# One block for three stages: feed-forward's first weights loaded and split inside the last state-space step, and the softplus at other units

## The reference

```python
x = x + cross_attention(layernorm(x), ctx, wq, bq, wk, bk, wv, bv, wo, bo)   # 16 heads, 2048 keys
x = x + attn(layernorm(x), ...)        # state space, then an MLP
x = x + ffn(layernorm(x), ...)         # shared matrix + two weighted experts that share one matrix

def attn(Z):
    xs, z = split(Z @ in_proj_w.T)                         # 1024 channels each
    u = silu(causal_conv4(xs) + conv_b)
    dt_low, Bm, Cm = split(u @ x_proj_w.T)                 # 32 + 16 + 16
    dt = softplus(dt_low @ dt_proj_w.T + dt_proj_b)
    h[t] = exp(dt[t] * A) * h[t-1] + dt[t] * Bm[t] * u[t]  # 16 states per channel
    y = sum_n h[t, n] * Cm[t, n] + u * D
    Zm = rmsnorm((y * silu(z)) @ out_proj_w.T + Z, norm1_w)
    h1 = gelu(Zm @ mlp_w1.T + mlp_b1)                      # 2048 wide
    return rmsnorm(h1 @ mlp_w2.T + mlp_b2 + Zm, norm1_w)
```

## Time and profile before

| | |
|---|---|
| median of 3 runs | 4025.98 us (4024.71 to 4027.25) |
| profiled execution | 4028.83 us |
| its span, first to last instruction | 4027.1 us |
| granted TensorE clock, mean | 0.986 of full |
| PE busy | 3844.0 us, 95% |
| DVE busy | 2824.2 us, 70% |
| ACT busy | 1744.4 us, 43% |
| POOL busy | 1273.4 us, 32% |

### The profile page before, as it was taken

How to read it: one execution, slowest core, us unless ns; L and a number is a source line. 1 busy time by engine, 2 the same in 40 slices (tenths; PEclk the granted TensorE clock), 3 DMA queues, 4 the chain that set the end, 5 groups by cost and what they waited for, 6 DMA issues and landing times. The chain is left out here.

```text
span 4027.1 us, 83594 instructions
## 1 busy us (share of the span) xinstructions
PE 3844.0 (95%) x34880; PEld 2814.3 (70%) x34880; DVE 2824.2 (70%) x2977; ACT 1744.4 (43%) x3482; POOL 1273.4 (32%) x599
## 2 busy tenths in 40 slices
PE   8999999999999999999999998999999997699998
PEld 6777777877777777777777775555545553388886
DVE  5667667657667766766766766999999999654443
ACT  2324324414423433432442445776777767222221
POOL 1111111011011111111111103888888889521011
PEclk9999999999999999999999998999999999799999
DMA  4110110110010011111011022111211111220000
GB/s 154 38 43 29 38 43 28 38 53 31 28 50 31 29 51 37 35 38 43 28 38 43 28 83 89 53 30 45 63 58 58 32 42 48 76 74 22 32 23 20
DMA packets 96917, 183.73 MB, mean 46 GB/s; under 512 B 8465, under 2 KB 12945, under 8 KB 96562
## 3 DMA queue, kind: packets, MB, share of 16 engines
q1 hardware_dynamic: 96562, 178.27, 13.6%
HBM read 152.82 MB, written 25.43 MB: 44 GB/s over the span
## 5 line engine op out<-in xcount | busy, mean ns | idle before, releaser
L244 POOL TENSOR_TENSOR c_lo<-c_raw,c_hi 128x2048 fp32r<-128x2048 f32 x64 | 294.6, 4604 | 1973.8 <-DVE c_hi L346 1973.8
L434 DVE TENSOR_TENSOR prob_sums<-prob_sums,probs 128x1024 f32<-128x1024 f32 x480 | 566.6, 1222 | 116.4 <-ACT probs L319 116.4
L996 POOL TENSOR_TENSOR b_drive<-b_dt_u,b_bc 128x1024 f32<-128x1024 f32 x256 | 600.6, 2361 | 117.4 <-PE b_y L1433 83.6
L407 DVE TENSOR_REDUCE max_parts<-scores 128x2 f32<-128x1024 f32 x512 | 601.5, 1217 | 40.2 <-PE scores L571 40.2
L319 ACT ACTIVATE probs<-scores 128x512 f32<-128x512 f32 x1024 | 529.0, 603 | 216.3 <-PE scores L602 214.8
L399 DVE SCALAR_TENSOR_TENSOR k_lo<-scores,bk_sb,k_hi 128x512 fp32r<-128x512 f32 x256 | 192.2, 751 | 565.5 <-ACT k_hi L304 565.5
L1433 PE MATMUL b_y<-b_drive,b_ident 128*128 128x512 f32 x1024 | 501.9, 621 | 68.8 <-DVE b_drive L1296 40.1
L1285 DVE TENSOR_TENSOR_SCAN b_decay<-b_decay,b_drive 128x1024 f32<-128x1024 f32 x214 | 489.9, 2289 | 20.5 <-ACT b_decay L1151 18.9
L304 ACT ACTIVATE k_hi<-scores,bk_sb 128x512 fp32r<-128x512 f32 x256 | 176.4, 689 | 604.5 <-PE scores L523 604.5
L312 ACT COPY v_sb<-scores 128x512 f32<-128x512 f32 x240 | 141.2, 588 | 667.7 <-PE scores L523 667.7
L1151 ACT ACTIVATE b_decay<-b_dt,b_a 128x254 f32<-128x254 f32 x1024 | 425.3, 462 | 0.4
(11 more groups left out here) (232 smaller groups left out, 6518.5 us busy)
## 6 DMA issues: line engine op xcount, KB each, us to landing
c_raw<-in_ctx SPq DMA_DIRECT2D x64, 1024.0 KB, 5.1
b_bc<-bc_scratch SPq DMA_DIRECT2D x128, 256.0 KB, 4.4
q_scratch<-v_sb SPq DMA_DIRECT2D x4, 1024.0 KB, 4.3
q_raw<-q_scratch SPq DMA_DIRECT2D x16, 256.0 KB, 5.1
q_raw<-in_x SPq DMA_DIRECT2D x16, 256.0 KB, 2.8
x_scratch<-q_raw SPq DMA_DIRECT2D x16, 256.0 KB, 5.7
attn_scratch<-attn_out_sb SPq DMA_DIRECT2D x16, 256.0 KB, 2.0
b_attn<-attn_scratch SPq DMA_DIRECT2D x8, 512.0 KB, 5.5
```

Of the source, the lines that this page charges most:

```text
L244: pool.tensor_tensor(c_lo[:, slot], c_raw[:], c_hi[:, slot].bitcast(F32), ALU.subtract).then_inc(c_lo_ready, 1)
L407: dve.tensor_reduce(max_parts[:, g, 2 * pair:2 * pair + 2, s], max_banks[:, 2 * pair:2 * pair + 2, :], AX.X, ALU.max).then_inc(max_taken, 1)
L434: dve.tensor_tensor(part, part, probs[:, u % 4], ALU.add).then_inc(summed, 1)
L996: pool.tensor_tensor(drive[:, m % 4], dt_u[:, 2 * p:2 * p + 2, :].unsqueeze(1).to_broadcast([P, SG, 2, T]), bc[:, g, 0].unsqueeze(2).to_br ...
```

## The change

- The three stages are in one block. `feed_forward` returns its functions like the others. The last output projection, the last `add_input`, the squares, the weighing and the scaling of the last state-space step are handed to feed-forward's engine programs and are issued between its first instructions.
- In the last state-space step SP loads the eight pieces of `w1` (`load_first`, from unit 1 on), ACT makes the high parts (units 8 to 15, `high_w1`), POOL four low parts (units 14, 17, 20, 23) and the other four behind the loop. `b1` and the first two `zm` tiles are loaded after unit 25. The store of the `zm` of the step before the last (`zm_v[i - 1]`) stands behind all of these on SP.
- `w1`, `w2` and `w_shared` are split in place: the raw data lie where the low part goes. `w2` is loaded once the last unit is added, two pieces at a time, as before.
- To make room on POOL, the last step gives it four C products in place of seven (`POOL_C_LAST`).
- In every step `PE_DT`'s second half goes from unit 20 to 21, `take_t` from 21 and 24 to 22 and 25, the exponentials from 22 and 25 to 23 and 28, the rounding from 23 and 29 to 24 and 30, and POOL's first rounding error from 25 to 26.
- In attention the semaphore of the `bo` load is the one of the three other biases, so that ACT also waits for it before its first `take_queries`.

```diff
-            sp.dma_start(bo_rows[:], bo.partition_broadcast(P)).then_inc(bo_loaded, 16)
+            sp.dma_start(bo_rows[:], bo.partition_broadcast(P)).then_inc(bias_loaded, 16)
...
-            pool.wait_ge(bo_loaded, 16)
+            pool.wait_ge(bias_loaded, 4 * 16)
...
-            act.wait_ge(bias_loaded, 3 * 16)
+            act.wait_ge(bias_loaded, 4 * 16)
...
-    PE_HEADS, PE_OUT_LAST, PE_TURN, PE_IN_X, PE_X, PE_DT = (0, 2), 3, 6, (8, 9, 10, 12), 16, (18, 20)
+    PE_HEADS, PE_OUT_LAST, PE_TURN, PE_IN_X, PE_X, PE_DT = (0, 2), 3, 6, (8, 9, 10, 12), 16, (18, 21)
-    POOL_LOW = (25, 31)
+    POOL_LOW = (26, 31)
-    ACT_Z, ACT_DBC, ACT_ABS, ACT_EXP = (18, 20, 26, 29), 19, (21, 24), (22, 25)
-    ACT_ROUND, ACT_LOG0, ACT_GATE = (23, 29), 27, 4
+    ACT_Z, ACT_DBC, ACT_ABS, ACT_EXP = (18, 20, 26, 29), 19, (22, 25), (23, 28)
+    ACT_ROUND, ACT_LOG0, ACT_GATE = (24, 30), 27, 4
-    POOL_C, POOL_C_LAST = (10, 11, 12, 16, 19), (10, 13, 16, 19, 22, 25, 28)
+    POOL_C, POOL_C_LAST = (10, 11, 12, 16, 19), (9, 12, 26, 28)
...
+                else:
+                    sp.wait_ge(dt_ready, i * 2 + 1)
+                    sp.wait_ge(z_product, steps * pairs)
+                    load_first(lambda unit: sp.wait_ge(scanned, i * units + unit + 1),
+                               lambda unit: sp.wait_ge(summed, i * units + unit + 1 + 4))
                 if not first:
                     sp.wait_ge(zm_ready, i)
                     sp.dma_start(zm_v[i - 1], mix[:]).then_inc(zm_stored, 16)
...
+    ACT_SQUARES, ACT_XF, ACT_EXP, ACT_SCALE = 1, 7, 10, 2
+    ACT_HIGH, POOL_LOW, LATE = (8, 9, 10, 11, 12, 13, 14, 15), (14, 17, 20, 23), 25
...
+        def load_first(sp, wait_for_scan, wait_for_sum):
+            for n in range(pieces):
+                wait_for_scan(1 + n)
+                if n >= 2:
+                    sp.wait_ge(w1_loaded[n % 2], n // 2 * 16)
+                sp.dma_start(w1_raw[:, :, piece_cols(n)], w1_v[:, :, piece_cols(n)]).then_inc(w1_loaded[n % 2], 16)
+            wait_for_sum(LATE)
+            sp.dma_start(b1_sb[:], b1).then_inc(b1_loaded, 16)
             sp.dma_start(zm[:, 0], zm_v[0]).then_inc(zm_loaded, 16)
...
             sp.wait_ge(zm_loaded, 16)
             sp.dma_start(zm[:, 1], zm_v[1]).then_inc(zm_loaded, 16)
+
+        def high_w1(act, m):
+            if m in ACT_HIGH:
+                n = ACT_HIGH.index(m)
+                act.wait_ge(w1_loaded[n % 2], (n // 2 + 1) * 16)
+                act.copy(w1_hi[:, :, piece_cols(n)], w1_raw[:, :, piece_cols(n)]).then_inc(w1_high, 1)
+
+        def low_w1(pool, n):
+            cols = piece_cols(n)
+            pool.wait_ge(w1_high, n + 1)
+            pool.tensor_tensor(w1_lo[:, :, cols], w1_raw[:, :, cols], w1_hi[:, :, cols].bitcast(F32),
+                               ALU.subtract).then_inc(w1_split, 1)
...
+        def run_sync(sp, store_last_zm):
+            sp.sem_inc(out_stored, 16)
+            for n in range(2):
+                load_w2(sp, n)
+            for n in range(2, pieces):
+                sp.wait_ge(w2_split, n - 1)
+                load_w2(sp, n)
+            store_last_zm()
...
+            for n in range(len(POOL_LOW), pieces):
+                low_w1(pool, n)
...
+            low_w2(0)
+            low_w2(1)
+            weigh_last()
+            for n in range(2, pieces):
+                low_w2(n)
...
             take_zm(0)
-            act.wait_ge(consts_loaded, CONSTS_LOADED)
+            take_last_squares()
+            act.wait_ge(b1_loaded, 16)
...
                     if first:
+                        if m == ACT_SCALE:
+                            scale_last()
                         continue
...
-            for n in range(2):
-                split_weights(n)
-            split_zm(0)
+            split_zm(0)
+            add_last_input()
+            for n in range(2):
+                high_w2(n)
...
                         if m % piece == 0 and m // piece + 2 < pieces:
-                            split_weights(m // piece + 2)
+                            high_w2(m // piece + 2)
...
             turn_zm(0, 0, False)
+            project_last_out()
```

More of the change, by code:

```diff
@@ L910, in finish, with store_last_zm @@
             def finish():
+                sp.wait_ge(summed, steps * units + 4)
+            run_steps(sp, front, body, finish)
+            def store_last_zm():
                 sp.wait_ge(zm_ready, steps)
@@ L1019, in body, with run_scalar @@
                             make_dt_u(j, 1 - par, 0)
-            run_steps(pool, front, body, lambda: weigh_out(steps - 1))
-        def run_scalar(act):
+                    else:
+                        in_last_step(m)
+            run_steps(pool, front, body, lambda: None)
+            return lambda: weigh_out(steps - 1)
+        def run_scalar(act, in_last_step):
             act.wait_ge(ready, 7)
@@ L1187, in body @@
                         take_z(j, 1 - par, ACT_Z.index(m))
[L1189 to L1193, removed]
+            run_steps(act, front, body, lambda: None)
+            return lambda: take_squares(steps - 1), lambda: scale_out(steps - 1)
         FRONT_LINKS = group + pairs * (taps - 2)
@@ L1309, in body @@
                     assert chain.n == FRONT_LINKS, chain.n
[L1311 to L1315, removed]
+            run_steps(dve, front, body, lambda: end_pair(steps - 1, 1, pairs - 1))
+            return lambda: add_input(steps - 1, 1, True)
         def run_tensor(pe, values_last, attention_done):
@@ L1452, in body, with sum_added, feed_forward @@
                         project_out(i, par, PE_OUT.index(m), last)
-            def finish():
-                project_out(steps - 1, 1, pairs - 1, True)
-            run_steps(pe, front, body, finish)
+            run_steps(pe, front, body, lambda: None)
+            def sum_added(eng):
+                eng.wait_ge(sum_ready, steps * group)
+            return lambda: project_out(steps - 1, 1, pairs - 1, True), sum_added
         return run_sync, run_gpsimd, run_scalar, run_vector, run_tensor
-def feed_forward(nc, x1_dram, zm_dram, w1_t, b1, w2_t, b2, norm_w, w_gate, w_shared_t, w_expert_t, bias, out):
+def feed_forward(nc, x1_dram, zm_dram, w1_t, b1, w2_t, b2, norm_w, w_gate, w_shared_t, w_expert_t, bias, out, semaphores):
     batches, _, width = x1_dram.shape
@@ L1650, in body @@
                                    ALU.add).then_inc(zm_biased, 1)
+                if first:
+                    low_shared()
                 pool.wait_ge(squared, (t + 1) * group)
@@ L1658, in _, with run_scalar @@
             run_steps(pool, body)
-        @block.scalar
-        def _(act):
+        def run_scalar(act, take_last_squares, scale_last):
             act.sem_inc(h_ready, 2)
@@ L1852, in body @@
                         finish(i - 1, DVE_OUT.index(m))
-                assert chain.n == (pieces if first else TAIL_LINKS), chain.n
+                assert chain.n == (0 if first else TAIL_LINKS), chain.n
                 if not last:
@@ L1857, in _ @@
             run_steps(dve, body)
-            chain.base, chain.n = (steps - 1) * TAIL_LINKS + pieces, 0
+            chain.base, chain.n = (steps - 1) * TAIL_LINKS, 0
             add_mlp(steps - 1, 1)
@@ L1897, in second_product @@
                     pe.wait_ge(mix_ready, i * group + group)
+                    if first:
+                        sum_added(pe)
                 if first and m % piece == 0:
@@ L1967, in _ @@
                 expert(steps - 1, b)
+        early = load_first, first_low_w1, high_w1
+        return early, (run_sync, run_gpsimd, run_scalar, run_vector, run_tensor)
 def perceiver_layer(nc, i, out):
```

189 lines of the change are left out of this document (94 added, 95 removed).

## The result

| | before | after |
|---|---|---|
| median, us | 4026.61 (4024.71 to 4028.31) | 4000.03 (3999.69 to 4004.19) |
| profiled execution, span | 4027.1 | 3997.6 |
| seven state-space steps (pair end of step 0 to that of step 7) | 874.39 | 874.95 |
| last state-space step, to its last pair end | 86.71 | 86.58 |
| from there to feed-forward's first product | 30.83 | 7.14 |

What follows compares the result with a forecast made beforehand. DVE (120.4) and PE (119.4) were taken as near their limit in a 125.5 us state-space step. Terms -9.0 + 0.0 - 23.3 - 3.8 = -36.1 us took the median from 4025.98 to 3989.9, range 3984 to 3998.

Steps and rivals of the forecast that it cites:

- The softplus: Seven state-space steps: new units remove DVE's wait for ACT at unit 22, gaining 1.3 us each, -9.0 us.
- 0 "if another engine takes it all": Bound of the softplus term: no gain if another engine takes it all; the other bound was 9.9 us.
- rival B: Softplus gains nothing, because PE or a new ACT stall at unit 24 or 30 takes it: 3999, chance 0.15.
- The last step: Last state-space step: returned C products +3.8, late scans +3.5, PE waits -7.7, clock +0.4; sum 0.0 us.
- The lower bound of -1.7: Last state-space step: lower end of the range -1.7 to +5 around its forecast of 0.0 us.
- The seam: Between state space and feed-forward: PE starts the first product at 3483.4 instead of 3506.70, -23.3 us.
- Feed-forward's first step: 51.8 us instead of 55.6, with POOL and DVE colliding and a 3.6 us PE gap: -3.8 us.
- The allowance of 1.0 us for the clock: Feed-forward's first step: 1.0 us added for a clock that a 3.6 us gap may lower.
- rival D: No collision at the seam (4.3 us less) and the last step at its best: 3984, chance 0.13.
- Attention: ACT's wait for the bo load before its first take_queries costs nothing, with 2.0 us of cover.
- What I had at nothing: Feed-forward's later steps, forecast to stay as they were.

Runs made afterwards that it cites:

- Experiments 1 and 3: 1: softplus's new units alone in kernel before, 0.9997. 3: both halves of third z projection behind unit 23, changed kernel 0.9902, kernel before 1.0000.
- Experiment 6: Changed kernel, still one block, but w1 loaded and split only behind the state space's last sum: 4007.02 us, 0.9959.
- Experiment 5: Changed kernel with POOL's weighing behind its split of w2's piece 4 instead of 1, ACT's scaling behind product 10 instead of 2: 3996.02 us, 0.9927.
- experiment 2: Half a z projection behind unit 24 instead of 22: kernel before 1.0018, kernel before with softplus's new units 0.9990, changed kernel 0.9930.
- experiment 4: Changed kernel with POOL's four splits in the last state-space step behind units 16, 19, 22, 25 instead of 14, 17, 20, 23: 3999.26 us.

## Why the prediction was wrong

**The softplus (-9.0 forecast, between +0.6 and -0.9 measured).** The bounds of the term held, 0 "if another engine takes it all", and rival B gave 3999 for it. The step that failed is the sentence that DVE meets PE again "where it waits for the head projection". Between unit 22, where the wait was, and that projection in the next step there is another meeting, the end of pair 2 at unit 24, and PE's idle time that I added up (1.09 at unit 25, 0.2 at unit 29) lies behind it. Reserve behind a meeting place doesn't help ahead of it. The answer stood in the trace of before, PE's sum of unit 23 and the pair end that needs it:

```profile
3077.24 1.90 PE L1433 MATMUL b_y<-b_drive,b_ident 128*128 128x512 f32 x4
...
3079.21 0.67 DVE L1247 TENSOR_TENSOR b_gate<-b_y,b_gate 128x512 f32<-128x512 f32 x1
```

3077.24 + 1.90 = 3079.14, and DVE began at 3079.21: a margin of 0.07 us. No wait was printed, so I read it as no constraint. The view of the earlier trace rows also held a line that I left out when I wrote that DVE waits 0.7 us for PE. It is twice the end of a pair, at unit 8, and says that the two engines meet at such ends:

```profile
DVE b_gate L1247 <- PE b_y L1433: 1.4, 2, 0.7
```

Experiments 1 and 3 settle this: the units alone give 0.9 us or less, PE's projection alone gives nothing, both give 9.8 to 11 us. The mechanism and the size of the term were right, for a kernel with one more edit.

**The last step (0.0, measured -0.1).** Right in its parts: +1.2 and +2.3 forecast for scans 12 and 15, 1.20 and 2.21 measured; two waits at pair ends gone; a low clock in between. The last end grew from 4.16 to 5.60 us; it is 4.0 where the clock didn't fall ahead of it. A single pair of executions could not show 0.1 us: this step took 83.0 to 87.0 us in the six executions with the old code in it, mean 85.7, and 85.0 to 86.6 in five with the new, mean 85.6. The lower bound of -1.7 in the prediction isn't worked out from anything it shows.

**The seam (-23.3, measured -23.1 in place, -23.7 from the last pair end).** First product forecast for 3483.4, measured 3483.64. Experiment 6 adds what the sum left open: it is the block and the early input, hardly the early weights. The block and the early input weren't tried apart.

**Feed-forward's first step (-3.8, measured -4.2).** 51.8 us forecast, 51.43 measured, with a gap of 3.6 forecast and 3.31 measured and h_lo at 2.5. The allowance of 1.0 us for the clock was not used in this execution and was 1.4 in the four others with this code, 52.85 to 52.87. The old code took 53.35 to 56.00 us in six executions, so by the means (55.1 and 52.6) the term is -2.5: the mechanism was right, and that -4.2 lies so near -3.8 is in part luck. The 4.3 us that rival D takes off for the collision are 4.1 by the terms of the prediction, 0.5 + 3.6. The row of DVE's cast agrees with what the Trainium skill says under SBUF — State Buffer, SBUF: two separate sides: the operation that comes second on the shared port waits for the whole of the first. A cast of 0.69 us took 2.77. Experiment 5 shows that the order of the queue on POOL, not the collision alone, made two of the 3.3 us.

**Attention (0).** The span up to the state space's first timed pair end is 2514.97 instead of 2514.77. That fits 0, though with 5.5 us between executions it can't show it to better than that; ACT's first `take_queries` starts at 23.60 instead of 23.68, behind PE as before.

**What I had at nothing.** Feed-forward's seven later steps take 60.78 us each instead of 61.03 (in the kernel before, the first of them 60.95), nearly to the hundredth in every kernel on either side: 1.4 us in the six that have a next one, 2.3 with the last and the tail. That last 0.8 isn't established: last step and tail take 97.85 and 98.40 us in the two profiles of the changed kernel alone. Part of the 0.25 us a step is in the shared products, four 128x512 rows of 1.07 us instead of 1.09 or 1.10, and in the second products that stand alone at the step's end. The change moved feed-forward's tensors in SBUF and in PSUM; the order in PSUM is excluded, the places in SBUF weren't tried. It stays open.

The range of 3984 to 3998 reached to rival B less 1 us. 0.15 for B was too little for a term whose own bound was 0 and which made a quarter of the sum: with a margin of 0.07 us in the rows it had to be the likeliest case, and the forecast 3999. That this is within 1 us of 4000.03 would have been luck too: in the profiled pair everything but the seven steps came to -30.3 against -27.1 forecast, and the medians lie 2.9 us closer together than that pair.

## What to carry to other kernels

When a wait is removed, walk on from it to the next place where the freed engine meets each other engine, and work out the margin there from ends and starts; a row without a wait can have a margin of 0.07 us. Only idle time ahead of that meeting counts. Where two engines are busy nearly all the time (here 119.4 and 120.4 of 125.4 us), expect waits in pairs: each edit alone may measure as nothing, and it is the two together that are to be tried, with an eye on who consumes what was moved (2.40 us of ACT in experiment 2, about 1.2 us a step lost). When blocks are joined, ask separately for the join and for the early loads: here the join, with the early input, was worth 22 us at the seam and the early weights 8 to 9 behind it, less the 0.5 that their splits cost ahead of it. Before a part of a profile is held against a forecast, look how much the same part varies between executions of the same code.

## What the runs showed of the hardware

**The clock falls behind some gaps and not others, with the same instructions.** Every one of the seven steps has a gap of 2.67 us on PE ahead of its sum at unit 7. In the profile of the changed kernel the granted clock fell behind it in three of the seven, in the other execution of the same kernel in four, only one of them the same. Three of the rows of the first, and the 7.8 us from the start of each (the clock is the number ahead of the last two):

```profile
2759.20 3.78 PE L1444 MATMUL b_y<-b_drive,b_ident 128*128 128x512 f32 x4 [2.67 <-DVE b_drive L1310]
...
2885.94 1.98 PE L1444 MATMUL b_y<-b_drive,b_ident 128*128 128x512 f32 x4 [2.67 <-DVE b_drive L1310]
...
3011.11 3.68 PE L1444 MATMUL b_y<-b_drive,b_ident 128*128 128x512 f32 x4 [2.67 <-DVE b_drive L1310]
```

```profile
2759.20:2767.00 7.80, 7.63 (x16) 3.87 (x16) 5.71 (x4) 5.86 (x16) 7.55 (x5) 0.60 0.11 40
2885.94:2893.74 7.80, 6.39 (x21) 3.27 (x22) 7.76 (x6) 6.31 (x18) 7.80 (x5) 1.00 0.11 40
3011.11:3018.91 7.80, 7.01 (x19) 3.49 (x20) 7.07 (x5) 5.86 (x16) 7.80 (x5) 0.78 0.11 40
```

In the first the low clock lasted longest: DVE waited 2.06 us at the next end of a pair, and the step took 127.3 us. In the third DVE waited 0.70, in the second not at all, and steps without the fall take 124.6 us (125.2 once, in experiment 4). The kernel before has the fall as well, in four of seven. What decides isn't shown. That is in part why the seven steps of the changed kernel vary between 873.5 and 875.1 us, the last one between 85.0 and 86.6, and feed-forward's first between 51.43 and 52.87 (before: 53.35 to 56.00 in six executions with the same code there). A forecast of such a stretch has that much room either way, whatever its sum says: a gap's price is its length, plus at times the waits behind a low clock, here 0.7 to 2.1 us in the steps and 1.4 in feed-forward.

**A lock can be cheap.** In experiment 5 DVE's h_lo was held to 2.5 us six times in feed-forward's first step, and PE waited for it twice, 0.42 and 1.32 us. POOL, on the other side, waited 1.63 us for a cast of DVE's four times, since DVE came to them late. The pair settled into 4.0 us for a piece, for which PE needs 5.6.
